# State-space convolution: states of odd channels on the other half of the partitions, carried sums in two halves, and products of zeros among the transposes

## What is computed

```
u = tanh_recurrence(x, cond_1024, Wx, Wh, b)              # 8 x 512 x 256
dt = exp(log_dt);  A = -exp(A_log)                        # 256 channels, 64 exponents
K[m, l] = sum_n C_re[m, n] * exp(dt[m] * A[n] * l)
y = causal convolution of u with K over the tokens, per channel
x = x + y + u * D
x = x + ffn(gated_recurrence(x, ...))
```

## Time and profile before

| | |
|---|---|
| median of 3 runs | 973.94 us (973.1 to 974.42) |
| profiled execution, its own time | 974.19 us |
| its span | 972.3 us |
| TensorE matmul busy | 924.3 us (95% of the span) |
| VectorE, ScalarE, GpSimd busy | 42%, 52%, 31% of the span |
| transposes of u | 379.30 to 388.10 us |
| convolution | 388.10 to 447.85 us |
| mean granted TensorE clock | 0.978 of full speed |

### The profile page before, as it was taken

How to read it: one execution, slowest core, us unless ns; L and a number is a source line. 1 busy time by engine, 2 the same in 40 slices (tenths; PEclk the granted TensorE clock), 3 DMA queues, 4 the chain that set the end, 5 groups by cost and what they waited for, 6 DMA issues and landing times.

```text
span 972.3 us, 64880 instructions
## 1 busy us (share of the span) xinstructions
PE 924.3 (95%) x28864; PEld 777.5 (80%) x28864; DVE 410.7 (42%) x781; ACT 506.3 (52%) x1735; POOL 299.1 (31%) x324
## 2 busy tenths in 40 slices
PE   7999999999999999999999998999899999999993
PEld 5888888888888888996444446788899999999993
DVE  1000010100001103553899799875564646556450
ACT  2444444444444446443876587134465656566551
POOL 3111111111111110650003463760045364554545
PEclk6799999999999999999999999999999999999997
DMA  2222222221111111111001110533357666675634
GB/s 89 83 92 87 95 93 87 100 85 33 35 40 36 35 33 28 66 76 57 0 1 39 49 56 22 184 116 108 127 132 162 133 157 119 151 146 127 134 40 53
DMA packets 69161, 80.34 MB, mean 83 GB/s; under 512 B 24225, under 2 KB 53558, under 8 KB 69122
## 3 DMA queue, kind: packets, MB, share of 16 engines
q1 hardware_dynamic: 54242, 62.18, 20.3%
q0 software_dynamic: 14592, 17.10, 10.7%
q10 hardware_dynamic: 288, 0.56, 0.2%
HBM read 44.16 MB, written 33.83 MB: 80 GB/s over the span
## 4 chain that ended last, share of the span: by engine, by line
PE 81%; issue 5%; ACT 4%; POOL 4%; DVE 3%; DMA 2%; POOLq 0%; SPq 0%; ACTq 0%; DVEq 0%
PE ps L516 19%; PE ps L811 16%; PE ps L508 9%; PE ps L825 8%; PE ps L677 8%; PE ps L489 6%; PE ps L727 3%; POOL slots_in L447 2%; PE ps L577 2%; ACT tok L879 2%; PE ps L590 2%; PE ps L736 2%; PE ps L599 2%; PE ps L494 2%; DMA slots_in<-tok,arena 1%
## 5 line engine op out<-in xcount | busy, mean ns | idle before, releaser
L516 PE MATMUL ps<-tok,wh 128*32 128x8 f32 x16384 | 255.2, 180 | 12.9 <-issue 3.5
L879 ACT ACTIVATE tok<-ps 128x8 f32<-128x8 f32 x1024 | 155.9, 177 | 204.0 <-PE ps L516 201.6
L516 PEld LDWEIGHTS ps<-tok,wh 128*32 128x32 f32 x16384 | 220.0, 113 | 48.0 <-ACT tok L879 25.2
L466 POOL DMA_INDIRECT out<-arena,dest x80 | 127.9, 1599 | 99.3 <-ACT arena L1030 76.9
L489 PE MATMUL ps<-zero 128*32 128x192 bf16 x1920 | 141.1, 255 | 0.0
L418 POOL TENSOR_TENSOR big<-tok,zero 128x128 f32 x64 | 29.0, 453 | 322.0 <-ACT tok L879 322.0
L811 PE MATMUL ps<-xgT_hi,ew_hi 128*128 128x320 f32 (+1 forms) x384 | 119.5, 311 | 3.2 <-DVE spare L1275 1.6
L811 PE MATMUL ps<-xgT_hi,ew_lo 128*128 128x320 f32 (+1 forms) x384 | 119.5, 311 | 0.0
L811 PE MATMUL ps<-xgT_lo,ew_hi 128*128 128x320 f32 (+1 forms) x384 | 119.0, 310 | 0.0
L1143 DVE TENSOR_TENSOR arena<-arena,pack 128x256 f32 x32 | 13.6, 426 | 246.3 <-ACT arena L884 246.3
L1381 DVE TENSOR_TENSOR mid<-mid,ps 128x320 f32<-128x320 f32 (+1 forms) x96 | 46.6, 486 | 107.0 <-ACT mid L1048 57.5
(11 more groups left out here) (206 smaller groups left out, 1643.5 us busy)
## 6 DMA issues: line engine op xcount, KB each, us to landing
slots_in<-mid SPq DMA_DIRECT2D x16, 645.0 KB, 3.7
mid<-slots_in SPq DMA_DIRECT2D x16, 645.0 KB, 4.2
arena<-in_ex_down SPq DMA_DIRECT2D x16, 384.0 KB
arena<-in_ex_gate SPq DMA_DIRECT2D x16, 352.0 KB
arena<-in_ex_up SPq DMA_DIRECT2D x16, 352.0 KB
xst<-in_x_steps SPq DMA_DIRECT2D x66, 64.0 KB, 1.8
xtok<-in_x_tok SPq DMA_DIRECT2D x16, 256.0 KB, 2.7
mid<-k_pad SPq DMA_DIRECT2D x32, 128.0 KB, 3.1
```

The source lines that it names most:

```text
L466: pool.indirect_dma_start(out=out[:, :], out_offset=bass.IndirectOffsetOnAxis(ap=dest[:, z, t:t + 1], axis=0), in_=yo[:, z, t], in_offset= ...
L516: last = nc.tensor.matmul(sums_at(bank, t, o)[Q * j:Q * j + Q], wh[:, k, columns(j, o)], hring[:, (n - 1) % (2 * G), k], start=False, stop ...
L879: nc.scalar.activation(hring[:, n, o], sums_at(n // G, n % G, o), ACT.Tanh).then_inc(s_h[o], 1)
```

## The change

- Odd channels change halves: their states of half k are computed into half 1 - k, in tiles (0, 64) and (64, 0). For this the decay tables dt_q, c_q and masks have the two halves of the odd channels swapped, and a second table dt_s holds the steps unswapped for the powers (one more 128-column part of pack, one more ScalarE exponential at the start).
- The states of a round lie in half a bank for even and half a bank for odd channels: banks 0 and 1 for z = 0, banks 6 and 7 for z = 1, in an order of channels given by place_of. The decays are laid out in the same order. A second clearing (banks 6 and 7) on VectorE waits for the first group of transposes.
- carried is cut in two: even channels ahead of block_states(1 - z), odd channels behind it, with a semaphore s_half from the first to the second. The number of its products is the same. The wait for the scan of the round now stands ahead of carried(z, 0).
- From group 1 on, each group of transposes is followed by one product of zeros, 128 x 128 by 256 columns in 16 bits.

```
@@ pack, on the host and in SBUF
-        sizes = (C * B, NST, 1, P + KP, P, IT, ...)
+        sizes = (C * B, NST, 1, P + KP, P, P, IT, ...)
...
+        def states_at(z):
+            return psf[:, 512 * 6 * z + 256:512 * 6 * z + 768]
+        def place_of(c):
+            return CP // 2 * (c % 2) + c // 2
@@ gpsimd
-                pool.tensor_tensor(pw[:, m % 2], dt_q[:, CP * m:CP * m + CP]...
+                pool.tensor_tensor(pw[:, m % 2], dt_s[:, CP * m:CP * m + CP]...
-            pool.wait_ge(s_dtm, 3)
+            pool.wait_ge(s_dtm, 4)
@@ tensor, transposes
                 last.then_inc(s_utr, 1)
+                if n == 1:
+                    pe.wait_ge(s_xc, 1)
+                if n >= 1:
+                    nc.tensor.matmul(ps[:, 0, 0:256], zero16[:, 0:P], zero16[:, 0:256], start=True, stop=True)
@@ tensor, block_states
                     for k in range(C):
-                        to = ps[rows_of_half(k), z, RB * c:RB * c + RB]...
+                        h, at = k ^ c % 2, RB * place_of(c)
+                        to = states_at(z)[rows_of_half(h), at:at + RB]...
...
-                                                ..., tile_position=(HB * k, HB * k))
+                                                ..., tile_position=(HB * k, HB * h))
@@ tensor, carried
-                for c in range(CP):
-                    for k in range(C):
+                for c in range(crossed, CP, 2):
+                    for h in range(C):
                         for odd in range(2):
-                            last = nc.tensor.matmul(to_tokens(z, c, k, odd), qd[rows_of_half(k), CP * z + c], xc[rows_of_half(k), z, c]...
+                            last = nc.tensor.matmul(to_tokens(z, c, h ^ crossed, odd), qd[rows_of_half(h), CP * z + c], xc[rows_of_half(h), z, place_of(c)]...
-                last.then_inc(s_qmm, 1)
+                last.then_inc((s_half, s_qmm)[crossed], 1)
@@ tensor, a round
                     stand(z)
                     own_block(z)
+                    pe.wait_ge(s_xc, m + 2)
                     pe.wait_ge(s_pe, m + 2)
-                    pe.wait_ge(s_xc, m + 1)
                     pe.wait_ge(s_uea, 2 * m + SLOTS - 1)
-                    stand()
+                    stand(z)
+                    carried(z, 0)
                     block_states(1 - z)
-                    pe.wait_ge(s_xc, m + 2)
-                    pe.wait_ge(s_uea, 2 * m + SLOTS - 2)
-                    stand()
-                    carried(z)
+                    pe.wait_ge(s_half, m + 1)
+                    stand(z)
+                    carried(z, 1)
@@ scalar
+            nc.scalar.activation(dt_s[:], dt_s[:], ACT.Exp).then_inc(s_dtm, 1)
@@ vector
-            nc.vector.memset(ps[:, 0:2]..., 0.0).then_inc(s_xc, 1)
+            nc.vector.memset(ps[:, 0:2]..., 0.0)
+            dve.wait_ge(s_utr, 1)
+            nc.vector.memset(ps[:, 6:8]..., 0.0).then_inc(s_xc, 1)
```

More of the change, by code:

```diff
@@ L70, in build @@
         h0g = sb("h0g", [P, C, B])
-        sizes = (C * B, NST, 1, P + KP, P, IT, KP * C * KP, 8, HB, RB, R + CT)
+        sizes = (C * B, NST, 1, P + KP, P, P, IT, KP * C * KP, 8, HB, RB, R + CT)
         pack = sb("pack", [P, sum(sizes)])
-        h0r, a_bc, a_q, dt_q, c_q, d_k, masks, consts, iota_t, resets_t, rows_to = [pack[:, sum(sizes[:n]):sum(sizes[:n + 1])] for n in range(len(sizes))]
+        h0r, a_bc, a_q, dt_q, dt_s, c_q, d_k, masks, consts, iota_t, resets_t, rows_to = [pack[:, sum(sizes[:n]):sum(sizes[:n + 1])] for n in range(len(sizes))]
         h0r = h0r.rearrange("p (c b) -> p c b", c=C)
@@ L232, in build @@
         s_own = sem("s_own")
+        s_half = sem("s_half")
         s_slot_tz = [sem("s_slot_tz0"), sem("s_slot_tz1")]
@@ L575, in block_states @@
                     for k in range(C):
-                        to = ps[rows_of_half(k), z, RB * c:RB * c + RB].rearrange("p (b t) -> p b t", t=NB)[:, :, 1:NB]
+                        h, at = k ^ c % 2, RB * place_of(c)
+                        to = states_at(z)[rows_of_half(h), at:at + RB].rearrange("p (b t) -> p b t", t=NB)[:, :, 1:NB]
                         last = nc.tensor.matmul(to, pw[rows_of_half(k), z, c], u_tok[rows_of_half(k), CP * z + c].rearrange("p (b t) -> p b t", t=NB)[:, :, 0:NB - 1],
-                                                start=True, stop=True, skip_group_check=True, tile_position=(HB * k, HB * k))
+                                                start=True, stop=True, skip_group_check=True, tile_position=(HB * k, HB * h))
                 last.then_inc(s_tmm, 1)
@@ L592, in own_block, with carried, stand @@
                 last.then_inc(s_own, 1)
-            def carried(z):
-                for c in range(CP):
-                    for k in range(C):
+            def carried(z, crossed):
+                for c in range(crossed, CP, 2):
+                    for h in range(C):
                         for odd in range(2):
-                            last = nc.tensor.matmul(to_tokens(z, c, k, odd), qd[rows_of_half(k), CP * z + c], xc[rows_of_half(k), z, c].rearrange("p (r e) -> p r e", e=2)[:, :, odd],
-                                                    start=False, stop=True, skip_group_check=True, tile_position=(HB * k, HB * odd))
-                last.then_inc(s_qmm, 1)
-            def stand():
-                nc.tensor.matmul(ps[0:Q, 6, 0:B], zero16[:, 0:Q], zero16[:, 0:B], start=True, stop=True, tile_position=(0, 0))
+                            last = nc.tensor.matmul(to_tokens(z, c, h ^ crossed, odd), qd[rows_of_half(h), CP * z + c], xc[rows_of_half(h), z, place_of(c)].rearrange("p (r e) -> p r e", e=2)[:, :, odd],
+                                                    start=False, stop=True, skip_group_check=True, tile_position=(HB * h, HB * odd))
+                last.then_inc((s_half, s_qmm)[crossed], 1)
+            def stand(z):
+                at = R * CP
+                nc.tensor.matmul(ps[0:Q, 2 + 2 * z, at:at + B], zero16[:, 0:Q], zero16[:, 0:B], start=False, stop=False, skip_group_check=True, tile_position=(0, 0))
             pe.wait_ge(s_uev, NB)
@@ L1446, with crossed @@
     masks = np.zeros((P, KP, C, KP), f32)
-    masks[:, np.arange(KP), :, np.arange(KP)] = (half[:, None] == np.arange(C))[None]
+    masks[:, np.arange(KP), :, np.arange(KP)] = (half ^ np.arange(KP)[:, None] % 2)[:, :, None] == np.arange(C)
     over = np.zeros((P, KP), f32)
+    def crossed(v):
+        w = v.reshape(C, P, -1).copy()
+        w[:, 1::2] = w[::-1, 1::2]
+        return w
     steps = x.reshape(B, S // G, G // 2, 2, C, P).transpose(1, 5, 4, 3, 2, 0).reshape(S // G, P, C, G, B)
@@ L1457 @@
     tri = np.stack([np.triu(np.ones((P, P)), 1) - 1, np.ones((P, P))], 1).astype(f32)
-    pack = (rows(cond.T), np.broadcast_to(a_log, (P, NST)), np.tile(a_log, C), np.concatenate([np.repeat(dt.reshape(C, P), HB, 0), over], 1),
-            c_re.reshape(C, P, NST).transpose(0, 2, 1), d_k, masks, consts, np.broadcast_to(-np.arange(HB, dtype=f32), (P, HB)),
+    pack = (rows(cond.T), np.broadcast_to(a_log, (P, NST)), np.tile(a_log, C), np.concatenate([np.repeat(crossed(dt)[:, :, 0], HB, 0), over], 1), np.repeat(dt.reshape(C, P), HB, 0),
+            crossed(c_re).transpose(0, 2, 1), d_k, masks, consts, np.broadcast_to(-np.arange(HB, dtype=f32), (P, HB)),
             np.broadcast_to((np.arange(RB) % NB > 0).astype(f32), (P, RB)),
```

12 lines of the change are left out of this document (7 added, 5 removed).

## The result

The changed kernel takes 1000.82 us (median of 4, 1000.36 to 1002.22) against 974.18 for the one before (973.1 to 980.24, 4 runs): ratio 1.0263, 95% interval 1.022 to 1.0306. It is slower, and far outside the range on record. The profiled execution has a span of 998.9 us. One thing has to be known for all that follows: an execution either keeps TensorE's clock through the convolution or loses it there, and the totals fall into two groups some 25 to 40 us apart; intervals given for kernels that do both compare the executions that kept it, while the ratio above sets 4 of after that all lost it against 4 of before that all kept it.

What follows compares the result with a forecast made beforehand. TensorE, busy for 95% of the span, was taken as the bound. -7.94 + 1.15 + 0.17 = -6.62 us gave a median of 967.3 us, with a range from 965.2 to 970.6 (a little over 8 in 10).

Steps and rivals of the forecast that it cites:

- The states on four tiles: Convolution: 32 pairs of a states block need 8 turns of 0.058 us instead of 16, over 17 blocks; -7.94 us.
- Order and waits: Within a convolution round: stands and carried sums cost the same and waits stay covered, scan slack 0.6 us; cost 0.
- the rival that waits are not covered: Convolution: s_half seen only after the states, or scan late, in each of 16 rounds; +4.3 us, 971.6; chance 9%.
- Products of zeros: Among the transposes: 14 added products at 0.109 us each, less 0.38 us free ahead of the copies; +1.15 us.
- cheap zeros: Rival, among the transposes: a product of zeros adds only 0.06 us; total 966.7 us; chance 20%.
- a drained array: Rival, among the transposes: each product of zeros drains the array; sum +2.6 us, total 976.6; chance 4%.
- The start: Kernel start: pack grows from 289 to 353 KB beside wx, which TensorE waits for; +0.17 us, bounds 0 and 0.66.
- The clock falls in one more stretch: Rival, in the recurrence's start or the experts: one more half-clock stretch costs up to 1.7 us, 969.0; chance 12%.
- The zeros' worth for the clock: Transposes and convolution: clock already 1.00 through both stages, so the zeros were given no gain from it.
- A: Experiments' theory, convolution: shorter states and the new order stream less through the array, and the clock falls by that.
- B: Experiments' theory: 15 added products move the program's seams and their stalls into a stretch that can't bear them.

Runs made afterwards that it cites:

- a_all: a_guard plus four products of zeros of 512 columns in the pause between transposes and first states; median 972.43 us of 11, 8 kept the clock (ratio of those 0.9952).
- a_guard: After, plus products of zeros ahead of second own block and following odd carried sums, first loop pass only; 6 of 10 kept the clock, those at ratio 0.9953.
- b_zeros: Before, with only the 15 products of zeros (256 columns) added among the transposes; 1012.33 us (4 runs), ratio 1.0378.
- b_pad2: Before, with 15 products of zeros of 8 columns among the transposes; 1012.69 us, one execution.
- a_no_zeros: After, without the products of zeros among the transposes; 1001.06 us, one execution.
- a_gap2: After, with four more products of zeros of 512 columns behind the last transposes; 1000.3 us, one execution.
- a_shift: After, with 112 tiny products of zeros added at the very start; 1003.56, 972.28, 1001.68, 999.66 us.
- a_align: After, without zeros among the transposes, three 512-column products behind the last transposes, two fewer warming products at the start; 1005.09, 1000.58, 968.06, 1003.86 us.
- b_zeros_shift: b_zeros with 112 more tiny products of zeros at the very start; 976.91, 1014.18, 979.92, 1013.49 us.
- a_hold2: After, with all 48 stands made two products of zeros of 256 columns; 984.91 us, one execution.
- a_align_fill: a_align with the stand ahead of each loop pass's second own block made two products of zeros of 256 columns; 1006.76, 969.25, 1002.5, 1007.77 us.

## Why the prediction was wrong

**The states on four tiles** (-7.94): right. 0.49 us for 32 pairs at full clock, two tiles on each row half with 56 columns. A pass of the loop takes 6.28 us (6.3 expected, 7.26 before), so a round is 0.49 us shorter, 0.04 of it at the end of the pass; with 0.42 for the first block, the term comes to 0.42 + 16 x 0.45 = 7.6 us. Two small errors cancel in it: the states got 0.58 shorter in a round and not 0.47, and cutting the carried sums in two, priced at 0, costs 0.14. The rule of the Trainium skill that was weighed there (TensorE: Matmul & The Clock Gate, Part 3, that weight loads overlap only across row groups) disagrees with this form too.

**Order and waits** (0): right. In a_all the scan starts at 405.01 and ends at 406.23, with the next carried sums at 406.93: slack 0.7 us where 0.6 was expected:

```profile
405.01 1.22 DVE L1204 TENSOR_TENSOR_SCAN arena<-arena,ps 128x512 f32<-128x512 f32 x1 [1.82 <-PE ps L595]
```

Only the first round lacks that cover, since no odd carried sums lie ahead of its own block; the step worked from a steady round and missed those 0.30 us. s_half shows no gap; the rival that waits are not covered falls.

**Products of zeros** (+1.15): right in size. The first states of after start at 389.38 instead of 388.18, +1.20 us. The rivals of cheap zeros and of a drained array fall.

**The start** (+0.17): nothing to be seen. pack lands in 3.2 us instead of 3.0, and the transposes begin at 379.3 as before; the lower bound was right.

**The clock**: the step that failed. The sum has no term for it: the prediction took the clock to stay at 1.00 through both stages. "The clock falls in one more stretch" was a rival of 12%, priced at up to +1.7 us by the one stretch of 3.5 us that the profile showed outside the start, and put in the recurrence or the experts. It fell in the convolution, for 82 us. Its price there: from 397.0 to 471.1 a round takes 5.12 us for 3.14, so 74.1 x (1 - 3.14 / 5.12) = 28.7 us, and the first gates add some: 8 products of 512 columns take 5.84 us, where before's rows have 3.70. The total is 998.9 against a forecast span of 967.3 - 1.9 = 965.4: 33.5 us. From the first states to the last carried sums after takes 81.7 us, where before has 59.6 and the forecast thus 51.7: 30.0 of the 33.5. The way from there to the end of those 8 products takes 9.3 instead of 6.4, another 2.9. What the change does where the clock stays is known only from its relatives; the lowest of a_guard, 969.05 us, has 1.35 us of filling in it.

The error had three parts. I took a level of 1.00 for a margin. I took the length of a fall from the nearest row, a place where dense products come next, when in the convolution the stream that loses the clock doesn't bring it back. And the sum has no term for the stalls of the first pass. The rows were taken from a steady pass, and the 0.14 us of "issue" in them, for which the prediction took "no change", is the end of the pass: it did not grow (0.06 to 0.10 in a_guard). The pause that grew was another, the 0.23 us at 393.67 in the first pass of before, which no row showed. It became 0.90 and 0.63 in after, 1.30 us more by themselves, and it moves with each instruction added ahead.

**The zeros' worth for the clock**: the prediction gave them nothing either way. Without them after lost the clock 7 us earlier, in one execution against one, so they may have bought time there. With them before lost it in 4 of 4 against 6 of 53 without: for before they did harm, and that is clear of chance.

**What is shown and what is not.** Shown: the lost clock is what makes after slow, by its profile and by relatives with few filling zeros, which take 968 to 974.5 us where they keep it; 15 products ahead of the convolution make before lose it (4 of 4 in b_zeros, and the one execution of b_pad2, where they stream next to nothing); and zeros ahead of both stalls help, as 14 of 21 executions of a_guard and a_all kept it against 2 of 14 of the kernels after, a_no_zeros, a_gap2, a_shift and a_align. Argued, not shown: that the stall is the way by which the 15 products act. They also start the convolution later, which no run has alone, and the seams put back gave 2 of 4. The zeros that fill the stalls stream as well, so they don't part A from B. That thin streaming alone is enough rests on one execution, and 1, 2 and 0 of 4 can't be told apart. Open: what decides between executions of one kernel; where the 7 of 21 lose the clock, as neither a_guard nor a_all was profiled in such an execution; and why stalls at one place differ in length (0.23 in before, 0.90 in b_zeros_shift). That faster code makes them longer can't be the only cause, since b_pad2 has 1.04 us in the slower code of before.

## What to carry to other kernels

Before a shortening is priced, look at what stands behind it at the same clock: a stretch of small tiles at 1.00 may be on the edge, and losing it costs the whole rest of the stretch, so its time belongs into the range even if the fall has never been seen there. Small gaps named "issue" inside a block of equal products were, as far as the runs here tell, seams of the program, and lay in the first pass of the loop, so rows of a steady pass don't show them. Instructions added ahead moved them, whatever they streamed. A kernel near the edge is timed over ten executions and not three. Where the entry of a loop is what fails, a few wide products of zeros in the first pass alone cost 1.35 us here (0.81 and 0.54 on the chain) and kept the clock in 14 of 21 executions: better odds, no cure.

## What the runs showed of the hardware that was not expected

A product of 8 columns among transposes costs what one of 256 does: a group of 4 with its product takes 0.55 us in both b_pad2 and after. The half clock at the start of the kernel lasts until 35 to 37 us in 12 of the 17 profiles, by the column or by the durations below, and until about 52 in those of a_hold2, a_all, a_shift, a_align and a_align_fill, for no reason that I found; the transposes then begin some 3 to 5 us later. And the granted clock of a profile can miss a fall. In a_guard and a_all the windows give 1.00 from the first us on, but up to 30 us a product of L499 takes 343 ns. In a_all it takes 344 still from 38 to 50 us, where after has 251:

```profile
L499 PE MATMUL ps<-zero 128*32 128x192 bf16 x52 | 4.8, 344 | 0.0
```
```profile
L499 PE MATMUL ps<-zero 128*32 128x192 bf16 x68 | 4.9, 251 | 0.0
```

So the clock is read from two places: the column, and the duration of one kind of product. In the convolution of a_guard and a_all both say full.
